# Writing finished expert blocks contiguously and gathering them per token tile on GpSimd, with every engine looped, in a one-core pre-norm recurrence and mixture-of-experts kernel

## The reference

```python
scores = sigmoid(xf @ gate_w.T)                      # 2048 tokens, 32 experts
# the 4 best of 8 groups of experts by their maximum, then the 6 best experts in them
w = w / sum(w) * 2.5
g = einsum('td,eid->tei', xf, w11); u = einsum('td,eid->tei', xf, w33)
y = einsum('tei,te,edi->td', silu(g) * u, c, w22)    # c holds w at the chosen experts
shared = silu(xf @ sw1.T) * (xf @ sw3.T) @ sw2.T
out = x + y + shared
```

## Time and profile before

| quantity | value |
|---|---|
| median of 3 runs | 449.61 us |
| the profiled execution's own time | 450.83 us |
| its span, first to last instruction | 449.1 us |
| mean granted TensorE clock | 0.89 |
| busy: PE, DVE, ACT, POOL | 376.1, 294.3, 260.7, 231.6 us |
| block loop, first transpose to last scaled block | 228.40 to 432.18 us |
| chain that ended last | PE 50%, DVE 19%, ACT 9%, DMA 8%, issue 8%, POOL 3% |

### The profile page before, as it was taken

How to read it: one execution, slowest core, us unless ns; L and a number is a source line. 1 busy time by engine, 2 the same in 40 slices (tenths; PEclk the granted TensorE clock), 3 DMA queues, 4 the chain that set the end, 5 groups by cost and what they waited for, 6 DMA issues and landing times.

```text
span 449.1 us, 9145 instructions
## 1 busy us (share of the span) xinstructions
PE 376.1 (84%) x2120; PEld 301.2 (67%) x2121; DVE 294.3 (66%) x990; ACT 260.7 (58%) x585; POOL 231.6 (52%) x242
## 2 busy tenths in 40 slices
PE   2777696965976778399889999999999998998935
PEld 2644263745645563155579999999999997997924
DVE  3669688999988824612235555555567777777982
ACT  2678978768575132011157777767777776776710
POOL 2000000752778777777516666666656665663750
PEclk9898867595785687689999999999999999999996
DMA  8990000220335999333347666666689889879724
GB/s 241 405 339 2 0 0 1 74 102 15 118 118 201 413 430 380 130 128 128 117 145 215 188 195 182 204 188 191 191 265 354 255 248 300 303 208 336 244 83 174
DMA packets 41850, 87.70 MB, mean 195 GB/s; under 512 B 7204, under 2 KB 32295, under 8 KB 41296
## 3 DMA queue, kind: packets, MB, share of 16 engines
q1 hardware_dynamic: 28384, 54.77, 36.7%
q0 software_dynamic: 10704, 30.07, 18.6%
q10 hardware_dynamic: 2720, 2.40, 1.7%
HBM read 49.81 MB, written 39.71 MB: 199 GB/s over the span
## 4 chain that ended last, share of the span: by engine, by line
PE 50%; DVE 19%; ACT 9%; DMA 8%; issue 8%; POOL 3%; DVEq 1%; SPq 1%; ACTq 0%; POOLq 0%
PE PS L1228 17%; PE PS L1235 8%; PE PS L1165 7%; DMA payload_and_xn_t<-choice_rows 5%; PE PS L1220 4%; PE PS L1121 3%; POOL choice_rows L441 3%; PE PS L1178 3%; DMA resid<-in_x 2%; PE PS L1076 2%; ACT L605 1%; DVE st L682 1%; PE PS L1261 1%; ACT payload_and_xn_t L555 1%; DMA choice_rows<-block_out_s,block_meta 1%
## 5 line engine op out<-in xcount | busy, mean ns | idle before, releaser
L441 POOL DMA_INDIRECT choice_rows<-block_out_s,block_meta x127 | 127.0, 1000 | 86.0 <-issue 58.3
L427 POOL DMA_INDIRECT bucket_rows<-payload_and_xn_t,dest x96 | 101.9, 1062 | 116.2 <-DVE dest L874 88.2
L1228 PE MATMUL PS<-block_rows_t,block_gate_up_weights 128*128 128x128 f32 x1016 | 134.9, 276 | 0.0
L1228 PEld LDWEIGHTS PS<-block_rows_t,block_gate_up_weights 128*128 128x128 f32 x1016 | 123.4, 192 | 1.1 <-ACT block_rows_t L630 0.9
L625 ACT ACTIVATE block_gate_up_weights<-expert_weights 128x512 f32 x127 | 80.0, 630 | 35.6 <-issue 29.6
L1235 PE MATMUL PS<-expert_weights,block_hidden_t 128*128 x254 | 76.3, 382 | 3.8 <-DVE block_hidden_t L985 3.8
L992 DVE TENSOR_SCALAR block_out_s<-PS,block_meta 128x256 f32<-128x256 f32 x127 | 61.2, 482 | 0.0
L985 DVE TENSOR_TENSOR block_hidden_t<-block_silu_t,PS 128x128 f32<-128x128 f32 x127 | 36.3, 286 | 24.2 <-ACT block_silu_t L617 22.0
L630 ACT ACTIVATE block_rows_t<-PS 128x256 f32<-128x256 f32 x127 | 46.5, 366 | 7.6 <-PE PS L1220 7.6
L1220 PE MATMUL PS<-ident,block_rows_s 128*128 128x128 f32 x254 | 48.6, 273 | 1.4 <-DVE resid L964 1.3
L980 DVE COPY block_meta<-block_rows_s 128x2 f32 x127 | 22.0, 173 | 41.7 <-issue 41.4
(11 more groups left out here) (185 smaller groups left out, 459.1 us busy)
## 6 DMA issues: line engine op xcount, KB each, us to landing
block_rows_s<-bucket_rows SPq DMA_DIRECT2D x127, 160.0 KB
payload_and_xn_t<-choice_rows SPq DMA_DIRECT2D x16, 768.0 KB, 6.5
bucket_rows<-pad_rows SPq DMA_DIRECT2D x1, 5120.0 KB, 26.3
expert_weights<-in_experts SPq DMA_DIRECT2D x1, 4224.0 KB, 14.0
expert_weights<-in_experts SPq DMA_DIRECT2D x1, 3456.0 KB, 16.3
expert_weights<-in_experts SPq DMA_DIRECT2D x1, 2688.0 KB, 18.3
resid<-in_x SPq DMA_DIRECT2D x4, 512.0 KB, 9.3
choice_rows<-block_out_s,block_meta POOLq DMA_INDIRECT x127, 3.2
```

Source lines behind the costliest of these rows:

```text
L427: nc.gpsimd.indirect_dma_start(out=bucket_ap[:, :], out_offset=bass.IndirectOffsetOnAxis(ap=dest[:, t, k:k + 1], axis=0), in_=PAY[:, t, :] ...
L441: nc.gpsimd.indirect_dma_start(out=choice_ap[0:rows, :], out_offset=bass.IndirectOffsetOnAxis(ap=meta_id[:, slot, 1:2], axis=0), in_=yy[:, ...
L1228: ins = mm(PS[:, 2 + r, g * P:(g + 1) * P], ws[:, r, (2 * k + g) * P:(2 * k + g + 1) * P], xT[:, r, k * P:(k + 1) * P], start=(k == 0), st ...
```

## The change

Finished blocks are no longer scattered. SP writes each one as 128 contiguous rows to a DRAM tensor ordered by expert (`write_block`, second transfer of SP in every step), and POOL gathers, for each of the 16 tiles and each of its 6 choices, 128 rows of 1 KB into a ring of four slots (`gather_outputs`, 96 indirect DMAs). The row numbers for the gathers are computed by DVE among the shared expert's work (`output_rows`, `output_sources`). The bucket row shrinks to 288 elements, 1152 bytes, and two DVE instructions per chunk in `choose` that made row numbers are gone. The output tensor is first cleared from the zero tile in five transfers of SP, 16.6 MB in all. There are nine phases instead of five (after 2, 4, 6, 8, 10, 12, 14, 15 and 16 tiles), so the table computation works on 288 columns instead of 160, and has four rows instead of three. Positions of the last two chunks come after the first of the shared expert's products, and two more such products come ahead of the table's transposition. All engines loop with 8 steps per turn up to step 120; DVE adds one choice per step from step 51 on in loops of 24 steps; SP stores the first eight tiles in loops of 24 steps; ACT stores nothing; PE sums no tile.

```diff
-    ROW = D + 2 * E
+    ROW = D + E
-    LP = 16
+    LP = 8
-    PHASE_ENDS = (1, 2, 3, 4, 5)
-    PH = len(PHASE_ENDS)
+    CUTS = [[2], [2], [2, 4], [2, 4], [2], [1, 2]]
+    PHASE_TILES = [b * TS + t0 + cut for (b, t0, nt), cuts in zip(CHUNKS, CUTS) for cut in cuts]
+    PH = len(PHASE_TILES)
-    RING = 6
...
+    LOOPED = BLOCKS // LP * LP
+    RING = 4
+    TURN_ADDS = RING * TOPK
+    FIRST_ADD = 51
+    ADD_TURNS = (BLOCKS + 2 - FIRST_ADD) // TURN_ADDS
+    FIRST_STORE = 72
+    STORE_TURNS = 2
+    WRITE_LAG = NXS + 3
...
         def blocks_through(phase):
...
+            return (PHASE_TILES[phase] * P * TOPK + E * (P - 1)) // P
...
+            for n in range(NCH - 1):
+                part = slice(n * BLOCKS // (NCH - 1), (n + 1) * BLOCKS // (NCH - 1))
+                sp.wait_ge(s_gp, n + 1)
+                sp.dma_start(outputs_ap[part.start * P:part.stop * P].rearrange("(j p) d -> p j d", p=P),
+                             PADT[:, 0:D].unsqueeze(1).to_broadcast([P, part.stop - part.start, D])).then_inc(s_clear, 16)
...
+            def load_block(j, u, taken):
+                if u % 4 == 0:
+                    sp.reg_load(first_rows, tabs[0:1, bass.ds(j, 4)])
                 if taken is not None:
                     sp.wait_ge(s_xtp, taken)
                     sp.wait_ge(s_meta, taken)
-                row = sp.value_load(tabs[0:1, bass.ds(j, 1)], min_val=0, max_val=E * CAP - P)
+                row = sp.snap(first_rows[u % 4], min_val=0, max_val=PLANE - P)
+                sp.dma_start(xs[:, u % NXS, :], bucket_ap[bass.ds(row, P), :]).then_inc(s_xs[u % NXS], 16)
...
+            def write_block(j, u):
+                if u % 4 == 0:
+                    sp.reg_load(first_outputs, tabs[0:1, bass.ds(j + 3 * P, 4)])
+                sp.wait_ge(s_y, j + 1)
+                row = sp.snap(first_outputs[u % 4], min_val=0, max_val=2 * P * P - P)
+                sp.dma_start(outputs_ap[bass.ds(row, P), :], yy[:, u % NY, :]).then_inc(s_ys[u % NY], 16)
...
+            with sp.Fori(2 * LP, FIRST_STORE, LP) as i:
                 for u in range(LP):
+                    load_block(i + u, u, i + (u - NXS + 1))
+                    write_block(i + (u - WRITE_LAG), (u - WRITE_LAG) % LP)
+            with sp.Fori(0, STORE_TURNS, 1) as turn:
+                for u in range(TURN_ADDS):
+                    j = turn * TURN_ADDS + (FIRST_STORE + u)
+                    load_block(j, u, j - (NXS - 1))
+                    write_block(j - WRITE_LAG, (u - WRITE_LAG) % LP)
+                    if u % (2 * TOPK) < 2:
+                        store_tile(u // (2 * TOPK) * 2 + u % (2 * TOPK), turn)
...
+            def gather_outputs(n):
+                all_written(pool, blocks_through(phase_of(n)))
+                pool.wait_ge(s_src, n // TS + 1)
+                if n < RING:
+                    pool.wait_ge(s_resid, B)
+                for k in range(TOPK):
+                    if n >= RING:
+                        pool.wait_ge(s_added, added(n - RING, k))
+                    nc.gpsimd.indirect_dma_start(
+                        out=RINGS[:, n % RING, k, :], out_offset=None, in_=outputs_ap[0:BLOCKS * P, :],
+                        in_offset=bass.IndirectOffsetOnAxis(ap=source[:, n, k:k + 1], axis=0)).then_inc(s_cin[n % RING][k], 16)
...
-                dve.wait_ge(s_memb, i + 1)
-                flat_memb = memb[:, CHUNKS[i][1]:CHUNKS[i][1] + nt, :].rearrange("p t e -> p (t e)")
-                c.add(V.tensor_tensor_scan(rank[:, n, :].rearrange("p t e -> p (t e)"), flat_memb, flat_memb, 0.0, AD, ALU.bypass))
-                c.wait()
-                c.add(STT(PAY_id[:, rows, D + 1::2], rank[:, n, :], float((NT - 1 - tile) * P * TOPK),
-                          idb[:, n].unsqueeze(2).to_broadcast([P, nt, E]), AD, AD))
...
+            def add_choice(n, k, turn=None):
+                slot = n % RING
...
+                    dve.wait_ge(s_cin[slot][k], turn * 16 + 16)
+                    dve.wait_ge(s_added, turn * TURN_ADDS + (added(n, k) - 1))
+                    total = resid_row[:, bass.ds(turn * (RING * D) + n * D, D)]
+                TT(total, total, RINGS[:, slot, k, :], AD).then_inc(s_added, 1)
...
+            with dve.Fori(0, ADD_TURNS, 1) as turn:
+                for u in range(TURN_ADDS):
+                    step(turn * TURN_ADDS + (FIRST_ADD + u), FIRST_ADD + u)
+                    add_choice(*divmod(u, TOPK), turn)
+            done = ADD_TURNS * TURN_ADDS
+            for s in range(FIRST_ADD + done, BLOCKS + 2):
+                step(s, s)
+                add_choice(*divmod(done, TOPK))
+                done += 1
+            for m in range(done, NT * TOPK):
+                add_choice(*divmod(m, TOPK))
...
             shared_gate_up(0, 0)
+            positions(4)
+            positions(5)
             pe.wait_ge(s_xn2, NCH)
             shared_gate_up(0, 1)
-            positions(4)
-            positions(5)
+            shared_gate_up(1, 0)
             pe.wait_ge(s_dest, NCH)
             pe.wait_ge(s_tabf, 3)
...
-            with pe.Fori(LP, UNROLL_AT, LP) as i:
+            with pe.Fori(LP, LOOPED, LP) as i:
...
-            pe.wait_ge(s_y, BLOCKS)
-            pe.wait_ge(s_fin, PE_SUM)
-            pe.wait_ge(s_cin[PE_SUM], 16)
-            for k in range(TOPK):
-                mm(PS[:, 0, 0:D], ident[:], RINGS[:, PE_SUM % RING, k, :], start=(k == 0), stop=False)
-            mm(PS[:, 0, 0:D], ident[:], resid[:, PE_SUM, :], start=False, stop=True).then_inc(s_sump, 1)
```

More of the change, by code:

```diff
@@ L390, in _ @@
+            for j in range(FIRST_STORE + STORE_TURNS * TURN_ADDS, BLOCKS):
+                load_block(j, j, j - NXS + 1)
+                write_block(j - WRITE_LAG, j - WRITE_LAG)
+            for j in range(BLOCKS - WRITE_LAG, BLOCKS):
+                write_block(j, j)
+            for n in range(LOOPED_STORES, NT):
+                store_tile(n)
+            sp.wait_ge(s_out, 16 * NT)
         @block.gpsimd
@@ L953, in _ @@
[L953 to L960 removed]
+            c.add(TT(tabf[:, 4:5], tabf[:, 0:1], j128[:, 0:1], AD))
@@ new lines, in _, with output_rows, each @@
+            dve.wait_ge(s_tabp, 1)
+            V.tensor_copy(tabs[0:1, :], PS[0:1, 3, 0:4 * P]).then_inc(s_tab, 1)
+            def output_rows():
+                full = BLK_I[1][:, 0:E]
+                first, shift = before_loop[:, 0:E], before_loop[:, E:2 * E]
+                def each(ap):
+                    return ap.unsqueeze(1).to_broadcast([P, NT, E])
+                c.wait()
+                c.add(STT(BLK_I[0][:, 0:E], cbs[:, PH, :], 0.0, cbs[:, 0, :], AD, SU))
+                c.wait()
+                c.add(TSC(full, BLK_I[0][:, 0:E], -P, None, ALU.bitwise_and))
+                c.wait()
+                c.add(STT(first, full, 1.0, cbs[:, 0, :], AD, AD))
+                c.wait()
+                c.add(STT(shift, first, float(P - 1), cbs[:, PH, :], AD, SU))
+                c.add(TT(SPLIT, dpos[:], each(first), ALU.is_ge))
+                c.wait()
+                c.add(TT(SPLIT, SPLIT, each(shift), M))
+                c.wait()
+                c.add(TT(SPLIT, SPLIT, dpos[:], AD))
+                c.add(STT(dpos[:], dpos[:], 0.0, each(OUT0), ALU.is_gt, M))
+                c.wait()
+                TT(dpos[:], dpos[:], SPLIT, AD).then_inc(s_added, 1)
@@ L962, in shared_out, with output_sources @@
+            def output_sources(g):
+                at_least(dve, s_src, g)
+                dve.wait_ge(s_added, 1)
+                for t in range(TS):
+                    c.add(V.max(dv[:, t, :], dpos[:, g * TS + t, :]))
+                c.wait()
+                TSC(source[:, g * TS:(g + 1) * TS, :], dv[:, :, 0:TOPK], -1.0, None, AD).then_inc(s_src, 1)
             def shared_out(b):
@@ L1024, in _ @@
+            for s in range(LP + 3):
                 step(s, s)
-            with dve.Fori(LP, UNROLL_AT, LP) as i:
+            with dve.Fori(LP + 3, FIRST_ADD, LP) as i:
                 for u in range(LP):
-                    step(i + u, u)
-            for s in range(UNROLL_AT, BLOCKS + 2):
-                step(s, s)
-                for n in range(NT):
-                    if n in ADD_AT and ADD_AT[n] <= s < ADD_AT[n] + TOPK // ADD_RATE[n]:
-                        for _ in range(ADD_RATE[n]):
-                            add_choice(*divmod(adds["done"], TOPK))
```

277 lines of the change are left out of this document (113 added, 164 removed).

## The result

| | median of runs | ratio to before |
|---|---|---|
| before | 450.11 us (448.42 to 450.67) | |
| changed | 460.79 us (459.08 to 466.12) | 1.0231, 95% interval 1.0178 to 1.0285 |

The change costs 10.7 us.

A forecast was written before the change was run, and what follows sets the result against it. PE's block loop (45% of the span, 1.546 us per step) was taken as the bound, with POOL's scatters ahead and a 16.9 us tail behind. -2.1 - 3.0 + 0.8 + 6.0 + 4.3 = +6.0 on 449.6 gave 455.6 us, range 445 to 466.

The forecast's parts named there:

- SP's issue rate, +6.0: Block loop: SP needs 1.55 us per step, 1.67 with stores, so writes, gathers and adds come late; +6.0 us.
- 2.4 us remain, so nothing waits: Block loop: gathers of a phase's last block have 2.4 us to spare before their add, if SP is on time.
- the -3.0 for the inner stalls: Block loop: PE's three inner waits for DVE's late product, behind adds waiting for 768 KB transfers, go; -3.0 us.
- The tail, +4.3: Behind the loop: POOL's 24 last gathers set the end, T + 21.2 against T + 16.9; +4.3 us.
- Start, -2.1: Ahead of the loop: PE ends earlier, POOL becomes late next, loop starts at 226.3 instead of 228.4; -2.1 us.
- the rival that the overlap does nothing: Ahead of the loop: POOL's scatters end it, so only 2.1 is lost, 457.7 us; inside the range, no own chance.
- ACT's and PE's turns, +0.8: Block loop: 14 turns instead of 3, 11 more edges at 0.07 us each; +0.8 us.
- Clearing, 0: Ahead of the loop: 16.6 MB in five transfers lie under nearly idle slices; cost 0, without that cover up to 41 us.
- DVE's adds, 0: Block loop: one add per step from 51, one fewer than before, outweighs added register work; cost 0, bound above 7 us.
- SP on pace (449.6): Block loop: SP's step is 1.42 us, stores under the slack, all but the 6.0 stays; 449.6 us, chance 0.22.
- cheap gathers: Tail: a gather costs POOL 1.0 instead of 1.27 us, 24 take 6.2 us less; 443 to 447, chance 0.20.
- dear register loads: SP's loop step: a four-register load costs four times one, 1.17 us, giving 496; over 466, chance 0.13.

The follow-up runs named there:

- The part alone: Kernel before with only the reordered start: last positions behind the first half product, four half products ahead of the table; 448.13 us, before 448.81, ratio 1.0013.
- both edits: Changed kernel with each block written one step of SP earlier and tile 12 gatherable after block 108; 455.02 us, before 448.36, ratio 1.0152.
- the earlier write alone: Changed kernel with writes two steps of SP earlier (9 blocks behind the loads), phases unchanged; 453.74 us, before 448.81, ratio 1.0124.

## Why the prediction was right and wrong

The range (445 to 466) held the time, the sign was right, and the sum was +6.0 for +10.7. By its steps:

- **SP's issue rate, +6.0: wrong.** SP takes 1.20 us for a load and a write. With the 0.21 for table loads that is 1.41, against the 1.55 I forecast and PE's 1.546. The failing terms are the load's 0.74 and the write's 0.60, put together from instructions and gaps: they are 0.66 and 0.54. That is little, but the forecast step stood exactly at PE's pace, and the whole 6.0 hung on the stores that came on top of it. The sign that I had named for it, SP waiting for DVE still, is there (13.2 us before its loads). The four-register load was rightly taken at the price of one. The Trainium skill, Runtime: NRT & Kernel Launch, section Instruction fetch mechanics, has about 200 ns per register and so 0.8 us for four, an estimate by that page, which speaks of register loads that the runtime injects; the table here lies in SBUF, the row has 0.299, and the trace decides. SP's writes are late for another reason: their order. With every write behind the next load, which waits for DVE, a block waits 3 us or more for its turn.
- **"2.4 us remain, so nothing waits", part of the -3.0 for the inner stalls: wrong, and by 6.0 us.** The stalls of before did go, but six others came, in four of the seven phases: without the first three steps the excess of 4.82 us became 7.80, +3.0 for -3.0. The margin was made of the landing of one transfer (2.1 us) and some 3 for the gather, which measured 3.1 to 5.8 and 3.7 to 5.7 at the loop's load. Two runs show the cause: one step less of lag (with the added phase) takes the waits from 5.7 to 1.4 us, and two steps less alone take them to 1.6. I had named the place ("the add, behind which the product of the next block is queued on DVE, and PE waits for that") with the wrong cause.
- **The tail, +4.3: right in kind, too small by 7.3.** POOL's 24 gathers are the bound, at 1.267 us where I had 1.27. They start at T - 10.6, not T - 13.3, for the same lateness of write and landing, and so the store lands at T + 23.4 instead of T + 21.2. The rest, 5.1 us, is the closing DRAIN, a term that I put at nothing without a reason: it had a row in the trace of before and cost nothing there.
- **Start, -2.1: not found.** PE was free early and POOL became late next, as said (PE waited 5.75 us for the first rows in the changed kernel); but POOL's last scatter started at 222.62, 1.9 later than before, and the profile's gain is 0.4, which the slower clock of the first three steps takes back. That PE pays for standing idle at the start was in no term of my sum. The part alone measured -0.9 to +2.2 us. This is the rival that the overlap does nothing, whose condition held; its 457.7 still has the 6.0 of SP in it.
- **ACT's and PE's turns, +0.8: not seen.** At the edges of turns the steps show nothing over 0.3 us in the trace with both edits, whose whole excess is 1.03 us. **Clearing, 0; DVE's adds, 0: held**, the first within some 3 us as above. It does not lie under empty slices alone (they are 4 to 7, and not 3 to 6 as I counted). The pace between waits is 1.546 us.

Of the rivals, SP on pace (449.6) had its premise and not its time; cheap gathers and dear register loads are refuted by 1.267 and 0.299 us. So the range was held partly by luck: a cost of 6.0 that did not exist stood in for 6.0 in the loop that the forecast had missed. The tail's shortfall, 7.3 us in the profiled execution, is more than the error of the total, 4.7 by the medians.

What is still lost after the earlier write alone is 0.0124 x 449 = 5.6 us, and the DRAIN outlasts SP's last landing by 4.9 us in that trace too. That it would be level with the kernel before if the DRAIN were short is arithmetic, not a measurement. No version run here beat the kernel before.

## What to carry to other kernels

Where one queue issues two kinds of transfer in turn, cost not only its rate but also the age of what it issues: a write that stands behind a load inherits the load's wait. A margin for a chain of write, gather and add needs each landing as the loop under load shows it, not the shortest in the trace. And when an engine's last work moves to the very end, its closing work, hidden until then, comes with it. Here it was longer as well, 8.9 us behind the last work where it was 2.0, which no row of before could tell.

## What the runs showed that was not expected

- POOL's closing DRAIN takes 8.9 to 9.0 us beyond POOL's last work in every profile of a kernel with gathers (twelve), whatever that work is (gather, memset, scatter; with a wait, 8.9 us from the wait's end), and ended 2.0 us after the last scatter in two profiles without them.
- Where PE had waited 5.75 to 6.84 us for the loop's first rows, its granted clock was 0.50 at the loop's start, and the first three steps took 1.4 to 2.7 us more than in the kernel before; after waits of 1.31 and 3.42 us it was 1.00.
- SP reads four registers from SBUF in 0.299 us, as fast as one.
- At some times all other engines run at a fraction of their pace while POOL issues gathers back to back: 583 us for the changed kernel, 534 for the one before, a ratio of 1.09 where it is 1.02 otherwise. Why, was not found.
